# Light and routing stage with nine descent rounds, the first heavy gather inside it, and four banks for the last token group's o and z products

## The reference

```python
def coor_descent(s, k, n_iters, eps):          # n_iters = 50, eps = 1
    logk = jnp.log(jnp.asarray(k, dtype=s.dtype))
    def step(ab, _):
        a, b = ab
        sb = (s + b) / eps
        a = eps * (logk - jax.scipy.special.logsumexp(sb, axis=-1, keepdims=True))
        b = -jax.nn.relu(s + a)
        return ((a, b), None)
    (a, b), _ = jax.lax.scan(step, (jnp.zeros_like(s[..., :1]), -s), None, length=n_iters)
    return jnp.exp((s + a + b) / eps)

light_out = feed_forward(x, light_gamma, light_w1, light_b1, light_w2, light_b2)   # 512 -> 256 -> 512
s = jnp.einsum('bnd,d->bn', x, routing_token)
scores = coor_descent(s, effective_k, N_ITERS, EPS)
sel_scores, sel_idx = jax.lax.top_k(scores, 512)
routed = jnp.take_along_axis(x, sel_idx[..., None], axis=1)
routed_out = feed_forward(routed, heavy_gamma, heavy_w1, heavy_b1, heavy_w2, heavy_b2)  # 512 -> 2048 -> 512
heavy_out = jnp.zeros_like(x).at[batch_idx, sel_idx].set(routed_out)
return light_out + heavy_out
```

## Time and profile before

| | us |
|---|---|
| median of 3 runs (lowest, highest) | 3545.03 (3543.87, 3550.61) |
| the profiled execution | 3546.22 |
| its span | 3544.4 |
| PE busy | 3320.6 (94%) |
| DVE busy | 2775.0 (78%) |
| POOL busy | 1957.7 (55%) |
| ACT busy | 1559.3 (44%) |

### The profile page before, as it was taken

One profiled execution on the slowest core, in us unless ns is written; L12 is line 12 of the kernel. 1 busy time (PEld: TensorE's weight loads), 2 busy tenths in 40 slices (PEclk: granted clock), 3 DMA queues, 4 the chain that ended last, 5 costly groups with the idle time before them and its releaser, 6 DMA issues. The chain is left out here.

```text
span 3544.4 us, 55654 instructions
## 1 busy us (share of the span) xinstructions
PE 3320.6 (94%) x17474; PEld 2570.6 (73%) x17474; DVE 2775.0 (78%) x5530; ACT 1559.3 (44%) x5385; POOL 1957.7 (55%) x1819
## 2 busy tenths in 40 slices
PE   8999999999779999999999799999999868889998
PEld 6777777777557777777777677777777556668886
DVE  3788888888577777777775589999999768767775
ACT  1766666666321111111111477777777534211111
POOL 1665565655346666666666466666666533223333
PEclk9999999999889999999999899999999989999999
DMA  7345455444275666666665545545554457420111
GB/s 206 101 143 157 133 141 158 139 140 144 93 213 149 159 160 164 165 163 159 159 160 115 146 112 158 160 134 148 158 163 120 121 192 263 179 90 13 24 18 24
DMA packets 284783, 491.00 MB, mean 139 GB/s; under 512 B 54018, under 2 KB 74818, under 8 KB 283778
## 3 DMA queue, kind: packets, MB, share of 16 engines
q1 hardware_dynamic: 243698, 408.87, 37.8%
q0 software_dynamic: 32256, 77.65, 11.5%
q10 hardware_dynamic: 8592, 1.57, 0.3%
HBM read 250.32 MB, written 136.96 MB: 109 GB/s over the span
## 5 line engine op out<-in xcount | busy, mean ns | idle before, releaser
L854 ACT ACTIVATE t_pr<-ps,t_negmax 128x154 f32<-128x154 f32 x2048 | 869.5, 552 | 336.3 <-DVE t_negmax L632 336.0
L563 POOL TENSOR_TENSOR t_pr<-t_pr,t_inv 128x616 f32<-128x616 f32 x512 | 639.9, 1250 | 537.2 <-DVE t_inv L647 534.5
L854 ACT ACTIVATION_READ_ACCUMULATOR t_pr<-ps,t_negmax 128x1 f32 x2048 | 481.8, 235 | 0.0
L655 DVE COPY t_pTm<-ps 128x512 f32<-128x512 f32 x512 | 350.0, 684 | 162.4 <-PE ps L929 161.7
L632 DVE TENSOR_REDUCE t_negmax<-ps 128x4 f32<-128x616 f32 x512 | 403.6, 788 | 21.9 <-PE ps L916 21.4
L928 PEld LDWEIGHTS ps<-ident,t_pr 128*128 128x128 f32 x2048 | 315.5, 206 | 133.2 <-issue 74.5
L916 PE MATMUL ps<-t_kst,t_stack 98*128 98x154 f32 x2048 | 353.7, 292 | 25.1 <-issue 11.1
L928 PE MATMUL ps<-ident,t_pr 128*128 128x128 f32 x2048 | 342.5, 290 | 19.8 <-DVE t_pTm L655 9.7
L916 PEld LDWEIGHTS ps<-t_kst,t_stack 98*128 98x128 f32 x2048 | 280.2, 194 | 39.0 <-issue 25.8
L80 PE MATMUL ps<-e_xT_high,e_wgu_high 128*128 128x512 f32 x768 | 305.4, 398 | 1.4 <-DVE e_xT_low L1423 1.4
L82 PE MATMUL ps<-e_xT_high,e_wgu_low 128*128 128x512 f32 x768 | 304.3, 396 | 0.0
(11 more groups left out here) (338 smaller groups left out, 8399.6 us busy)
## 6 DMA issues: line engine op xcount, KB each, us to landing
t_stack<-t_q_high SPq DMA_DIRECT2D x1016, 64.0 KB, 2.0
c_wgu_in<-in_gate_upT SPq DMA_DIRECT2D x32, 1536.0 KB, 11.4
t_stack<-t_q_low SPq DMA_DIRECT2D x512, 64.0 KB, 2.0
x_dram<-t_xs SPq DMA_DIRECT2D x32, 1024.0 KB, 5.5
c_wd_in<-in_downT SPq DMA_DIRECT2D x32, 768.0 KB, 12.9
xs_dram<-t_z SPq DMA_DIRECT2D x16, 1032.0 KB, 7.7
...
```

What stands on the lines that cost most here:

```text
L563: pool.tensor_tensor(p, p, inv[:, v, :].unsqueeze(1).to_broadcast([P, KEYS, HG]), ALU.mult).then_inc(s["normed"], 1)
L655: dve.tensor_copy(pTm[:, g % 2, :, t * P:(t + 1) * P], ps[:, 4, :].rearrange("p (h n) -> p h n", h=HG)).then_inc(s["pTm"], 1)
L854: op = act.activation(pr[:, u % 4, :, h], flat[:, col:col + KEYS], ACT.Exp, bias=negmax[:, u, h:h + 1], accum_out=total[:, u, h:h + 1])
```

## The change

- Last group's banks: in both token stages the four o tiles of group 15 go to banks 6, 0, 1, 2 (after all exponentials are done), and layer 0's four z chunks of group 15 to banks 3, 0, 1, 2, with no wait between them.
- The start of the light stage: SP issues w1 and gamma ahead of z of group 0; DVE makes w1's parts first and w2's after group 0's low parts and the chain's first seven steps; ACT waits for the biases later.
- Routing: 49 iterations in nine rounds of 6, 6, 6, 6, 5, 5, 5, 5, 5 instead of seven of 7, on groups 0 to 8. The paces are now 28 steps for groups 0 to 3, 24 for 4 to 8, 22 for 9 to 13, 15 for 14, and 1 for 15.
- Finding the rows: position = 128 x tile + lane. DVE compares the lane only, 8 columns of scores at a time (8 instructions of 1024 elements, `hot`), and spreads the two digits of each index over four tiles (2 instructions of 1024, `spread`). PE makes 64 matmuls with `hot` as weights and 32 columns, one after another, after `inner(15, 1)`. The result lies by partitions, so the last copy and transposes are gone. `vals` is now made by POOL.
- The row numbers are ready before `result(15, 3)`; POOL gathers batch 0's rows (into `c_xh0`) inside the light stage, and the heavy stage starts without a gather.

```diff
+        def o_bank(j, t):
+            return (A_BANK, 0, 1, 2)[t] if last(j) else A_BANK
+        def z_bank(j, k):
+            return (T_BANK, 0, 1, 2)[k] if last(j) else T_BANK
...
             def project(j, par, t, chunks, cur, nxt):
                 if 0 in chunks:
-                    if t == 3 and nxt:
+                    if t and last(j):
+                        pe.wait_ge(s["exped"], UNITS * NG)
+                    elif t == 3 and nxt:
...
-    ROUND, CLIP = 7, 20.0
-    ROUNDS = (ITERS - 1) // ROUND
+    SIZES, CLIP = (6, 6, 6, 6, 5, 5, 5, 5, 5), 20.0
+    ROUNDS = len(SIZES)
...
-            sp.dma_start(z[0][:], rows(scr["xs"], 0)).then_inc(s["z_in0"], 16)
-            sp.dma_start(w1_in[:], a["light_w1"].rearrange("(k p) n -> p k n", p=P)).then_inc(s["w_in"], 16)
+            sp.dma_start(w1_in[:], a["light_w1"].rearrange("(k p) n -> p k n", p=P)).then_inc(s["w1_in"], 16)
...
+                sp.dma_start(z[0][:], rows(scr["xs"], 0)).then_inc(s["z_in0"], 16)
...
+            pool.wait_ge(s["xb2"], TG * NG)
+            pool.wait_ge(s["rowed"], 1)
+            for n in range(CC):
+                pool.indirect_dma_start(
+                    out=c["xh0"][:, n, :], out_offset=None, in_=scr["xs"][:, :],
+                    in_offset=bass.IndirectOffsetOnAxis(ap=c["heavy_rows"][:, 0, n:n + 1], axis=0),
+                ).then_inc(c["xh0_in"], 16)
...
+                link(dve.tensor_tensor(past[:], pos[:].unsqueeze(2).to_broadcast([P, C, CC + 1]),
+                                       tile_edge[:].unsqueeze(1).to_broadcast([P, C, CC + 1]), ALU.is_ge))
...
+                link(dve.tensor_tensor(tile_hot[:], past[:, :, 0:CC], past[:, :, 1:CC + 1], ALU.subtract))
...
+                link(dve.tensor_reduce(tile_no[:], past[:, :, 1:CC], AX, ALU.add))
...
+                link(dve.scalar_tensor_tensor(pos[:], tile_no[:], -float(P), pos[:], ALU.mult, ALU.add))
...
+                    dve.tensor_tensor(spread[:, r], vals[:, r].unsqueeze(3).to_broadcast([P, C // 2, 2 * B, CC]),
+                                      tile_hot[:, r].unsqueeze(2).to_broadcast([P, C // 2, 2 * B, CC]),
+                                      ALU.mult).then_inc(s["spread"], 1)
...
-                for j in range(C):
-                    reached(dve, s["hot_mm"], j - RING + 1)
-                    dve.tensor_scalar(hot[:, j % RING, :], slots[:], pos[:, j:j + 1], None,
+                for j in range(0, C, PART):
+                    dve.tensor_tensor(hot[:, j:j + PART, :], lane[:].unsqueeze(1).to_broadcast([P, PART, P]),
+                                      pos[:, j:j + PART].unsqueeze(2).to_broadcast([P, PART, P]),
                                       ALU.is_equal).then_inc(s["hot"], 1)
...
             def paces(n):
-                    return (13, 7, 2, 2, 2, 1, 1, 0, 0, 4 if n + 1 < ROUNDS else 1)
...
+                    return (9, 6, 2, 2, 2, 1, 1, 1, 0, last) if SIZES[n] == 6 else (7, 5, 2, 2, 1, 1, 1, 1, 0, last)
...
+                mm = pe.matmul(ps[:, SIDE, 0:2 * B * CC], hot[:, j, :], spread[:, j].rearrange("p w n -> p (w n)"),
+                               start=(j == 0), stop=(j == C - 1))
...
                 inner(n, 1)
+                if n == 0:
+                    pe.wait_ge(s["w_low"], 2)
+                if n == FOUND_AT:
+                    found_rows()
...
-            for n in range(CC):
-                mm = pe.transpose(ps[:, SIDE, P + n * 2 * B:P + (n + 1) * 2 * B], found[:, n * P:(n + 1) * P],
-                                  c["ident"][0:2 * B, 0:2 * B])
...
-            gather(0, range(CC))
             low(0)
             low(1)
...
+            keep("xh0", [P, CC, XS])
```

More of the change, by code:

```diff
@@ L387, in x_bank, with last @@
             return FIRST[k] if isinstance(j, int) and j == 0 else T_BANK
+        def last(j):
+            return isinstance(j, int) and j == NG - 1
+        def o_bank(j, t):
+            return (A_BANK, 0, 1, 2)[t] if last(j) else A_BANK
+        def z_bank(j, k):
+            return (T_BANK, 0, 1, 2)[k] if last(j) else T_BANK
         def o_slot(par, k):
@@ L811, in z_turned @@
                     reached(act, s["part_mm"], j)
-                act.copy(zT[:, k, :], ps[:, T_BANK, :]).then_inc(s["zT_act"], 1)
+                act.copy(zT[:, k, :], ps[:, z_bank(j, k), :]).then_inc(s["zT_act"], 1)
             def part_out(j):
@@ L978, in project @@
                 for k in chunks:
-                    mm = product(pe, ps[:, A_BANK, :], [v[:, o_slot(par, k), t * P:(t + 1) * P] for v in oT],
+                    mm = product(pe, ps[:, o_bank(j, t), :], [v[:, o_slot(par, k), t * P:(t + 1) * P] for v in oT],
                                  [w[:, k, :] for w in wo], k == 0, k == DC - 1)
@@ L998, in z_turn @@
                         pe.wait_ge(s["xnT_low"], DC * (j + 3))
+                elif last(j):
+                    pass
                 elif k == 1:
@@ L1006, in z_turn @@
                     pe.wait_ge(s["zT_dve"], 2 * j + 2)
-                transposes(z, k, s["z_mm"])
+                transposes(z, k, s["z_mm"], z_bank(j, k))
             def gate_parts(j):
@@ L1632, in mixed_phase @@
     LOGK = math.log(EFF_K)
-    ROUND, CLIP = 7, 20.0
-    ROUNDS = (ITERS - 1) // ROUND
+    SIZES, CLIP = (6, 6, 6, 6, 5, 5, 5, 5, 5), 20.0
+    ROUNDS = len(SIZES)
+    assert sum(SIZES) == ITERS - 1
     DIGIT, WAYS = 3, 8
     STEPS = 11
-    RING = 14
+    PART = 8
     SIDE = 3
@@ L1820, in routing @@
                     dve.wait_ge(s["exped"], 2 * i + 2)
-                    for n in range(ROUND):
+                    for n in range(SIZES[i]):
                         linked()
@@ L1824, in routing @@
                         yield
-                        yield from over_rows(part[:], cap[:], 1.0 / EFF_K, "step" if n + 1 < ROUND else "capped")
+                        yield from over_rows(part[:], cap[:], 1.0 / EFF_K, "step" if n + 1 < SIZES[i] else "capped")
                     dve.wait_ge(s["logged"], i + 1)
@@ L2085, in outer, with found_rows @@
                     mm.then_inc(s["y_mm"], 1)
-            def found_rows(first, last):
-                for j in range(first, last):
-                    pe.wait_ge(s["hot"], j + 1)
-                    pe.matmul(ps[0:2 * B, SIDE, :], vals[:, j, :], hot[:, j % RING, :], start=(j == 0),
-                              stop=(j == C - 1)).then_inc(s["hot_mm"], 1)
+            def found_rows():
+                pe.wait_ge(s["spread"], 2)
+                for j in range(C):
+                    if j % PART == 0:
+                        pe.wait_ge(s["hot"], j // PART + 1)
+                    mm = pe.matmul(ps[:, SIDE, 0:2 * B * CC], hot[:, j, :], spread[:, j].rearrange("p w n -> p (w n)"),
+                                   start=(j == 0), stop=(j == C - 1))
+                mm.then_inc(s["hot_mm"], 1)
             for k in range(DC):
@@ L2141, in sb @@
             return ctx.enter_context(nc.sbuf_tensor(f"h_{name}", shape, dt))
-        xh = [sb(f"xh{q}", [P, CC, XS]) for q in range(2)]
+        xh = [c["xh0"], sb("xh1", [P, CC, XS])]
         xg = sb("xg", [P, CAP])
@@ L2155, in heavy_phase, with gathered @@
         block = ctx.enter_context(nc.Block())
+        def gathered(engine, b):
+            if b == 0:
+                engine.wait_ge(c["xh0_in"], 16 * CC)
+            else:
+                engine.wait_ge(s[f"gathered{b % 2}"], 16 * CC * ((b + 1) // 2))
         @block.gpsimd
@@ L2393, in build @@
             keep("heavy_rows", [P, B, CC], I32)
+            keep("xh0", [P, CC, XS])
+            c["xh0_in"] = part.enter_context(nc.semaphore("heavy_first_rows_in"))
             c["hw_in"] = part.enter_context(nc.semaphore("heavy_weights_in"))
```

86 lines of the change are left out of this document (45 added, 41 removed).

## The result

The changed kernel took 3532.7 us (median of 13 runs, 3518.58 to 3538.49), the kernel before, run beside it, 3550.16 us. The ratio is 0.9946 with a 95% interval of 0.9933 to 0.9958: about 19 us faster where 30 were forecast, and above the range of 3503 to 3529. The kernel before took 5.1 us more here than the 3545.03 from which the forecast started; 0.9946 of 3545.03 is 3525.9, so a part of the distance in absolute time is the level of these runs, not the change. The profiled execution took 3532.81 us, its span was 3531.1 us, 13.3 less than before. The two profiles show less than the medians do, because the profiled execution of the kernel before (3546.22) was 3.9 us under the median of its 13 runs.

The account below looks back on a forecast made before the run. Each light-stage group was taken to cost what the slower of PE and DVE needs. Terms +1.1 - 2.5 - 13.7 - 10.2 - 2.5 + 6.1 - 0.6 - 7.8 = -30.1 gave 3516.1 profiled, forecast 3515 us, range 3503 to 3529.

Parts of the forecast that it names:

- groups 4 to 8: Light stage, 24 steps each: two iterations fewer bring them to PE's floor, 14.2 us each, 71.0 against 84.7, -13.7.
- groups 13 and 14: Light stage: group 13 at 15.0 us, group 14 DVE bound at 19.6 with POOL, 34.6 against 37.1, -2.5.
- group 15 and end: Light stage's end: 64 products +4.7, row numbers +0.5, gather sharing DMA with the last store +0.9; +6.1.
- layer 0's tail: Token stage's last turns: no waits between o tiles, -2.0, and four z chunks without waits, -3.8.
- layer 1's tail: Token stage's last turns: two o tile waits gone ahead of the third residual, -2.0.
- Groups 9 to 12, the search: Light stage: 22 steps instead of 30, DVE bound at 16.4 us each; 66.4 with 0.8 for low clock against 76.6, -10.2.
- the search groups keep their clock loss: Rival: PE gaps keep groups 9 to 12 at 18.2 us, group 15's 64 products cost +2.6; 3525, chance 0.13.
- the steps were never the bound: Rival: the results' buffer cycle sets the pace, shorter chain gives nothing, only the ends move; 3538, chance 0.05.
- 22 to 24 us at worst: Group 14, if DVE's two-input instructions wait out each of POOL's four additions of 1.24 us whole.
- lower end of 0.03: Group 15's block: a 32-column product cannot be under 0.03 us, a tenth of a placement product; 0.119 was taken.
- estimate of 4 to 5 us: Group 15's block of 64 products at the skill's 60 to 81 ns each, against 7.6 us in the forecast.
- the barrier waits for POOL's four issues, not for their landing: End of light stage: the gather's issues should end inside the store's 5.7 us; sharing DMA engines costs +0.9.

Follow-up runs that it names:

- three other profiles: Changed kernel with batch 0's gather back in the heavy stage (0.9915), 1024-element compares moved from group 14 to 15 (0.9921), or the 64-product block four times (0.9954).
- Without collisions: Changed kernel with POOL's bias additions cut to one column instead of 512, so DVE does not meet POOL: 3519.88 us, ratio 0.9912.
- when placed later: Changed kernel, same 22 steps in groups 9 to 13, most moved from ahead of result(n, 0) to other places: 3522.66 us, ratio 0.9913.
- first combined kernel: Changed kernel with seven descent rounds, 17 re-placed steps per search group, compares five and three, block later, gather in heavy stage, z first: 3508.96 us, 0.9877.

## Why the prediction was wrong

The direction and the kind of gain were right (faster, the search and descent groups the largest part); the size was not. Of the 22.3 us forecast for the light stage and the heavy stage's start, 12.4 came:

| step of the sum | forecast | measured |
|---|---|---|
| start of the stage | +1.1 | +1.5 |
| group 0 | 0 | -1.7 |
| groups 1 to 3 | -2.5 | -0.8 |
| groups 4 to 8 | -13.7 | -11.3 |
| groups 9 to 12 | -10.2 | -4.8 here, -7.3 to -7.9 in three other profiles |
| groups 13 and 14 | -2.5 | +3.7 |
| group 15 and end | +6.1 | +2.3 |
| heavy stage's start | -0.6 | -0.9 to the first product, -1.3 to the first gelu |
| layer 0's tail, first residual to first gate | -5.8 | -3.1 here, -2.5 to -6.6 in ten profiles |
| layer 1's tail | -2.0 | -2.5 |

(Entries are differences of time stamps, rounded.) The two tails are right within the spread. The rest of the profile's gap to the forecast lies in unchanged code: from the first gate to layer 1's last o tiles 1759.9 us before, 1763.4 after, 1755.6 to 1765.6 in the ten others.

**The step that failed** is "Groups 9 to 12, the search": 19.6 - 8 x 0.40 = 16.4 us a group, "DVE bound", and with it group 14, "18.7 us, DVE bound", 19.6 with POOL. They took 17.9 and 23.2 us here (17.2 to 17.3 and 23.1 to 23.5 in other profiles of the same table). The sum of DVE's work was taken for a group's length, while the earlier trace rows already showed DVE busy only 56.78 of 76.60 us in groups 9 to 12 of the kernel before. In the changed kernel DVE was busy 14.65 us a search group, under the forecast's 16.4 and far under the 17.9. The runs put a loop in its place: a group lasts from split_h(n, 0) to result(n, 1) on DVE, and from there to split_h(n+1, 0) through outer(n, 2), outer(n, 3), inner(n+1, 0) on PE and the gelu on ACT. By the stamps of eleven profiles the second half is never under 7.2 us, whatever the table. Group 14: 3099.86 to 3113.33 is 13.5 us, then 9.7 to 3123.05, together 23.2. Without collisions it is 12.0 + 10.0. Steps in the first half lengthen the group; steps in the second first fill DVE's wait for the gelu. The changed table had 12 of 22 steps in the first half of search groups, and 7 when placed later; in the changed kernel that half took 10.1, 9.3, 8.8, 8.8 and 8.8 us in groups 9 to 13, with the steps later 7.3, 6.1, 6.0, 5.8 and 6.4. The second half, now with 15 steps, took 9.0 to 9.3 us in three of these five groups, so steps there are cheaper and not free, and the length came to 15.2, not to 13.2.

The first rival, "the search groups keep their clock loss", described the symptom: its 18.2 us per group is nearly what the four took (71.8/4 = 17.9). It should have had more than 0.13. Set against the kernel before of the same rounds, its 3525 is also the time that came (3525.9 above), and that is partly luck: its block of +2.6 on top of +4.7 never came, and its +7.2 should have been 6.4, as the forecast's 66.4 already held 0.8 for low clock. By its number the case "the steps were never the bound" (3538) was nearer to 3532.7 than this one, but its mechanism is refuted: the descent groups did gain.

The forecast's estimate by the Trainium skill, "SBUF — State Buffer", "Who interferes with whom", was 22 to 24 us at worst for group 14, and it was 23.2. The waits it names are in the trace (1.10 us for an instruction of 0.17), but the run without them had 22.0 us. The number was right and the reason mostly another. The compares of 1024 elements did not wait a whole addition: 1.70 instead of 1.22.

**Group 15** has two errors that partly cancel. From its gelu to the last store's issue it took 12.9 us before and 11.5 now, where the block and the row numbers were to add 5.2; from there to the heavy stage 5.66 and 9.38, 3.7 more where 0.9 was forecast. The block cost 0.028 us a product, not 0.119: 1.77 us in all, less than the 2.9 of the twelve products that went. The row used was fp32 and had fresh weights for one column; the prediction's lower end of 0.03 was right. The Trainium skill's page "TensorE: Matmul & The Clock Gate" ("Weight-path perf modes — Fast Weight Load (FWL) and DoubleRow", "Back-to-back issue gap") pointed the right way with the estimate of 4 to 5 us, still over twice what the trace shows. That estimate took the page's spacing for 128 moving columns; the block has 32. The sentence "the barrier waits for POOL's four issues, not for their landing" was false: POOL's DRAIN held the end until the gather had landed, and this cost 3.6 us.

**Groups 4 to 8** had a floor of 14.2 in the forecast and took 14.7. Groups 9 to 13 of the first combined kernel, with at most one step between z_low(n+1, 0) and result(n, 0), took 13.8 to 14.2, so the floor was right; that the steps there kept groups 4 to 8 above it is likely, but no run moved them.

**The expert slots.** In four of the ten profiles with the new tail and 50 idle transposes these ran at full clock throughout and took 5.65 us instead of 7.8. They ended over 4 us ahead of ctxT, and the key products took 19.3 to 19.6 us instead of 16.8. Where the products took 16.8 us with 50 transposes, the slots took 84.7 to 85.3 us, the kernel before included; where they took 18.5 to 19.6, 86.3 to 88.8. So part of the tail's gain was likely given back (84.9 us before, 86.5 on average in the eleven with the new tail), but no run isolates it.
